# Cross-attention kernel on one core: column sums of probabilities folded on DVE and summed by one float32r matmul per tile in place of a float32 one

## The reference

```python
# emb (16, 100, 512), latent (16, 722, 256), weights 512x512 and 256x512
q = jnp.einsum('bte,ef->btf', emb, Wq) + bq
k = jnp.einsum('bml,le->bme', latent, Wk) + bk
v = jnp.einsum('bml,le->bme', latent, Wv) + bv
w = jnp.einsum('bte,bme->btm', q, k) * scale
w = jax.nn.softmax(w, axis=1)
pred = jnp.einsum('btm,bme->bte', w, v)
x = pred + emb
...
return (x - mu) * jax.lax.rsqrt(var + EPS) * gamma + beta
```

## Time and profile before

| | us |
|---|---|
| median of 3 runs | 142.18 (141.69 to 142.43) |
| the profiled execution | 141.24 |
| its span, first to last instruction | 139.4 |
| busy PE, DVE, ACT, POOL | 133.3, 103.0, 88.0, 78.6 |

### The profile page before, as it was taken

How to read it: one execution, slowest core, us unless ns; L and a number is a source line. 1 busy time by engine, 2 the same in 40 slices (tenths; PEclk the granted TensorE clock), 3 DMA queues, 4 the chain that set the end, 5 groups by cost and what they waited for, 6 DMA issues and landing times.

```text
span 139.4 us, 3004 instructions
## 1 busy us (share of the span) xinstructions
PE 133.3 (96%) x1042; PEld 128.8 (92%) x1042; DVE 103.0 (74%) x208; ACT 88.0 (63%) x299; POOL 78.6 (56%) x77
## 2 busy tenths in 40 slices
PE   7999999999999999999999999999999999999940
PEld 7899999999998999999999999999999999998930
DVE  0789995893545789579696955969596966797983
ACT  4366188989978753988292839565656637386320
POOL 0000005579984695646989272965476553639791
PEclk9999999999999999999999999999999999999997
DMA  4999999984287596978969899599787987535324
GB/s 146 336 397 419 416 260 398 345 302 177 51 292 269 174 360 186 397 258 307 273 266 339 265 333 377 187 356 334 270 252 240 325 277 236 224 111 212 115 75 150
DMA packets 10814, 37.33 MB, mean 268 GB/s; under 512 B 1200, under 2 KB 1456, under 8 KB 10800
## 3 DMA queue, kind: packets, MB, share of 16 engines
q1 hardware_dynamic: 9424, 34.79, 71.6%
q10 hardware_dynamic: 1376, 2.36, 4.6%
HBM read 33.87 MB, written 3.28 MB: 266 GB/s over the span
## 4 chain that ended last, share of the span: by engine, by line
PE 89%; POOL 5%; issue 2%; ACT 1%; POOLq 0%; DVE 0%; DVEq 0%
PE ps_S L427 29%; PE ps_U L441 27%; PE ps_Y L462 10%; PE ps_U L399 6%; PE ps_Y L399 6%; POOL xT_in L990 3%; PE ps_Y L342 2%; POOL xT_in L978 2%; PE ps_w L450 1%; PE ps_S L347 1%; PE ps_U L508 1%; PE ps_c L416 1%; PE ps_U L353 1%; ACT xT_in L626 1%; PE ps_U L358 1%
## 5 line engine op out<-in xcount | busy, mean ns | idle before, releaser
L608 ACT ACTIVATE expo<-scores,negmax 121x100 f32<-121x100 f32 x96 | 34.9, 365 | 22.0 <-DVE negmax L779 22.0
L427 PE MATMUL ps_S<-G,ctxT_in 128*121 128x100 f32 (+1 forms) x384 | 43.3, 269 | 0.0
L427 PEld LDWEIGHTS ps_S<-G,ctxT_in 128*121 128x121 f32 (+1 forms) x384 | 42.1, 185 | 0.0
L441 PEld LDWEIGHTS ps_U<-prob,ctx_in 121*128 121x128 f32 x336 | 39.4, 192 | 1.0
L441 PE MATMUL ps_U<-prob,ctx_in 121*128 121x100 f32 x336 | 39.6, 274 | 0.0
L789 DVE TENSOR_REDUCE probsum<-prob 121x100 f32<-121x600 f32 x16 | 19.8, 1239 | 6.0 <-POOL prob L967 5.7
L978 POOL TENSOR_TENSOR xT_in<-x_in,xT_in 128x512 f32<-128x512 f32 (+1 forms) x13 | 16.6, 1280 | 13.3 <-issue 9.8
L775 DVE TENSOR_TENSOR scores<-ps_S,c_rows 121x600 f32<-121x600 f32 x16 | 12.5, 781 | 15.6 <-issue 12.2
L967 POOL TENSOR_TENSOR prob<-expo,rinv 121x600 f32<-121x600 f32 x16 | 19.0, 1189 | 0.1
L608 ACT ACTIVATION_READ_ACCUMULATOR expo<-scores,negmax 121x1 f32 x96 | 18.0, 187 | 0.0
L990 POOL TENSOR_TENSOR xT_in<-wqk,beta_rows 128x512 f32<-128x512 f32 (+1 forms) x12 | 15.4, 1280 | 2.7 <-ACT wqk L634 2.7
(11 more groups left out here) (125 smaller groups left out, 202.4 us busy)
## 6 DMA issues: line engine op xcount, KB each, us to landing
ctx_in<-ctx SPq DMA_DIRECT2D x16, 768.0 KB, 5.2
ctxT_in<-ctxT SPq DMA_DIRECT2D x16, 722.0 KB, 5.0
xT_in<-xT SPq DMA_DIRECT2D x8, 400.0 KB, 8.7
x_in<-x SPq DMA_DIRECT2D x12, 256.0 KB, 4.5
out<-xT_in ACTq DMA_DIRECT2D x8, 256.0 KB, 3.7
wqk<-Wqk SPq DMA_DIRECT2D x4, 388.0 KB, 4.4
out<-xT_in SPq DMA_DIRECT2D x3, 256.0 KB, 2.0
wv_in<-Wv SPq DMA_DIRECT2D x1, 512.0 KB, 15.5
```

What stands on the lines that cost most here:

```text
L427: last = nc.tensor.matmul(ps_scores(c)[0:rows(c), :], ctxT_in[:, q, l * M + c * MP:l * M + c * MP + rows(c)], G[:, l, bass.ds(b * T, T)], ...
L441: last = nc.tensor.matmul(ps_U[:, q, l * T:(l + 1) * T], ctx_in[0:rows(c), q, c, l * P:(l + 1) * P], prob[0:rows(c), q, c * T:(c + 1) * T] ...
L608: last = nc.scalar.activation(expo[0:MP, q, c * T:(c + 1) * T], scores[0:MP, q, c * T:(c + 1) * T], ACT.Exp, bias=negmax[0:MP, q, c:c + 1] ...
```

## The change

weight_sum(j) now multiplies a new array sum_parts (128 partitions by 128 tokens, float32r, two buffers) by ones in one float32r matmul with two columns, in place of probsum by ones in float32 with one column. DVE makes sum_parts in three new instructions per tile: fold_sum(j) adds partitions 64 to 120 of probsum onto partitions 0 to 56 in place; upper_sum(j) copies the 64 folded rows, rounded to float32r, into partitions 0 to 63; lower_sum(j) subtracts that copy from the folded rows into partitions 64 to 127. The last tile's weight_sum stands on PE behind the values of the tile before it, not ahead of them.

```diff
+        sum_parts = sb("sum_parts", [P, 2, P], F32R)
...
             def weight_sum(j):
-                pe.wait_ge(probsum_set, last_batch(j) + 1)
+                pe.wait_ge(sum_parts_set, j + 1)
                 if j > 0:
                     pe.wait_ge(wsum_set, j)
-                nc.tensor.matmul(ps_w[0:tile_rows(j), 0:1], probsum[0:MP, tokens(j)], ones[0:MP, 0:1],
+                nc.tensor.matmul(ps_w[0:tile_rows(j), 0:2], sum_parts[:, j % 2, 0:tile_rows(j)], ones_r[:, 0:2],
                                  start=True, stop=True).then_inc(wsum_done, 1)
...
             late_U(1)
-            weight_sum(NT - 1)
...
             last.then_inc(Y_done, 1)
+            weight_sum(NT - 1)
             late_U(2)
...
+            def fold_sum(j):
+                dve.wait_ge(probsum_set, last_batch(j) + 1)
+                nc.vector.tensor_tensor(probsum[0:MP - P // 2, tokens(j)], probsum[0:MP - P // 2, tokens(j)],
+                                        probsum[P // 2:MP, tokens(j)], ALU.add).then_inc(sum_folded, 1)
+
+            def upper_sum(j):
+                dve.wait_ge(sum_folded, j + 1)
+                if j >= 2:
+                    dve.wait_ge(wsum_done, j - 1)
+                nc.vector.tensor_copy(sum_parts[0:P // 2, j % 2, 0:tile_rows(j)], probsum[0:P // 2, tokens(j)]).then_inc(sum_hi_set, 1)
+
+            def lower_sum(j):
+                dve.wait_ge(sum_hi_set, j + 1)
+                nc.vector.tensor_tensor(sum_parts[P // 2:P, j % 2, 0:tile_rows(j)], probsum[0:P // 2, tokens(j)],
+                                        sum_parts[0:P // 2, j % 2, 0:tile_rows(j)].bitcast(F32), ALU.subtract).then_inc(sum_parts_set, 1)
...
             def turn(b, q):
                 j = tile_of(b - 3)
+                i = tile_of(b - 2)
                 if exists(b - 3):
                     lower_U(b - 3, 1 - q)
+                if i is not None:
+                    fold_sum(i)
                 normaliser(b - 1, 1 - q)
+                if i is not None:
+                    upper_sum(i)
                 maxima(b, q)
+                if i is not None:
+                    lower_sum(i)
...
             normaliser(0, 0)
             maxima(1, 1)
             chunk_sum(0, 0)
+            fold_sum(0)
             normaliser(1, 1)
+            upper_sum(0)
+            lower_sum(0)
             maxima(2, 0)
```

More of the change, by code:

```diff
@@ L166, in xattn @@
         probsum_set = sem("probsum_set")
+        sum_folded = sem("sum_folded")
+        sum_hi_set = sem("sum_hi_set")
+        sum_parts_set = sem("sum_parts_set")
         U_done = sem("U_done")
@@ L870, in _ @@
             chunk_sum(1, 1)
+            fold_sum(1)
             maxima(3, 1)
+            upper_sum(1)
             normaliser(2, 0)
+            lower_sum(1)
             dve.wait_ge(rows_in, 48)
@@ L883, in _ @@
             chunk_sum(3, 1)
+            fold_sum(2)
             centre(1)
+            upper_sum(2)
             lower_U(2, 0)
+            lower_sum(2)
             normaliser(4, 0)
@@ L895, in _ @@
             lower_U(B - 4, 0)
+            fold_sum(NT - 3)
             normaliser(B - 2, 0)
+            upper_sum(NT - 3)
             maxima(B - 1, 1)
+            lower_sum(NT - 3)
             add_residual(NT - 4)
@@ L900, in _ @@
             chunk_sum(B - 2, 0)
+            fold_sum(NT - 2)
             aggregate(NT - 4)
+            upper_sum(NT - 2)
             lower_U(B - 3, 1)
+            lower_sum(NT - 2)
             normaliser(B - 1, 1)
@@ L924, in _ @@
             chunk_sum(B - 1, 1)
+            fold_sum(LAST)
             add_residual(NT - 3)
+            upper_sum(LAST)
             late_lower(1)
+            lower_sum(LAST)
             row_stats(NT - 3)
```

## The result

The changed kernel takes 148.57 us (median; 147.92 to 148.98) against 141.95 (141.68 to 142.43) measured beside it: ratio 1.0476, 95% interval 1.0447 to 1.0506. The forecast was 150.4 us, in a range of 144.5 to 153.5, and a difference of +8.3 us; the difference is +6.6. Of every kernel, executions over 1.5% above its fastest are left out of medians and ratios.

The account below looks back on a forecast made before the run. PE's gapless matmuls bound the kernel; 4.5 + 0.5 (busy turns) + 1.3 (early) + 3.1 (tail) - 1.1 (PE's gain) = +8.3 us, so 150.4 us for the median, range 144.5 to 153.5.

Parts of the forecast that it names:

- What bounds, and the sign: PE's matmuls, busy 96% of the span, bound the kernel; the change makes it slower, chance 0.84.
- The fold and the lower part wait for the end of a POOL instruction: DVE's new two-SBUF-input instructions, coming second, wait for POOL's whole instruction; fold 1.3 to 1.6 us instead of 0.30.
- The cast waits as a whole: DVE's upper part also waits for POOL's instruction, 1 us instead of 0.22; case of both kinds waiting: chance 0.50.
- The rival in which it doesn't: Only the two-input DVE instructions wait, the cast doesn't: +0.85 us a turn, +5.0 in all, 147.2 us; chance 0.25.
- Turns 7, 11 and 12 at 1.5 us each, plus 0.5: Busy turns behind another busy turn: PE loses 1.5 us each, 4.5 together, and 0.5 more in turn 7.
- The 0.5 for L1006 and L1009: Turn 7: two POOL additions of 1.0 us each behind the probabilities catch the lower part, +0.5 us.
- Turns 8 and 13 ... turns 9 and 14: Turns without a tile of b - 2, or without values: DVE catches up there, PE's earlier loss stays.
- Early, 1.3 us: fold(0) waits behind POOL's Wv_lo, delaying DVE by up to 2 us; 1.3 us (0 to 3) reaches PE in turns 4 to 6.
- Tail, 3.1 us: From turn 15 on, waits of fold, cast and lower part delay DVE's L816 from 129.75 to 132.9: +3.1 us.
- PE's gain, 1.1 us: One float32r pass saves 0.11 us per weight sum, ten of 13 sums before the last scores end: -1.1 us.
- The last weight sum ... hidden: Moved behind values(11) on PE, it is ready at about 132.2, its residual wanted at 133.7: no cost.
- PE: gaps ... ahead of values: Expected sign in the profile: PE gaps of 1 to 2 us ahead of values in turns 8, 12 and 13.

Follow-up runs that it names:

- e4: Kernel before, with one float32r two-column matmul per weight sum on a constant array of ones, no new DVE work: 139.90 us, ratio 0.9894.
- e10: Kernel before, with the chunk sum itself writing float32r and one float32r matmul per weight sum, lower parts left out: 140.37 us, ratio 0.9907.
- e1: Changed kernel with fold, cast and lower part each turned into a one-input tensor_reduce over an axis of length one: 142.48 us, ratio 1.0070.
- e2: Changed kernel with only the cast turned into a tensor_reduce over an axis of length one: 146.98 us, ratio 1.0364.
- e7: Changed kernel with tile 0 summed the old way (float32, no new DVE instructions): 149.31 us, ratio 1.0557.
- e11: Changed kernel measured once more without any edit, in another set of runs: 148.73 us, ratio 1.0524.
- e6: Changed kernel with the last two tiles, 11 and 12, summed the old way (float32, no new DVE instructions): 145.96 us, ratio 1.0314.
- e3: Changed kernel with fold and lower part turned into tensor_reduces over an axis of length one, the cast kept: 142.63 us, ratio 1.0077.
- e8: Changed kernel with the three DVE instructions of tiles 1 to 10 moved behind the completing chunk sum, tiles 0, 11, 12 the old way: 144.02 us, ratio 1.0174.
- e9: As e8, but with the instructions of tiles 3, 6 and 10 moved behind the next turn's lower_U: 146.88 us, ratio 1.0384.

## Why the prediction was right, and where it was off

- **What bounds, and the sign: right.** PE was the bound, its gain is about 1% (e4, e10), and DVE's new work made it wait.
- **The fold and the lower part wait for the end of a POOL instruction: right**, and shown by the rows and by e1. "The fold in busy turns: 1.3 to 1.6 us long" was too long: it took 1.07 to 1.12.
- **The cast waits as a whole: right** (1.17 us). The rival in which it doesn't falls. e2's 146.98 is close to the 147.2 of that rival, which was its time for exactly that kernel.
- **Turns 7, 11 and 12 at 1.5 us each, plus 0.5: oversized.** Net of the 0.11 for PE the forecast is 1.9, 1.4 and 1.4, together 4.7; measured, as what values of turns 8, 12 and 13 lose, are 1.5, 0.8 and 1.2, together 3.5. DVE's turn came out at 8.0 us, not 8.3, mostly because the residual began 0.15 us earlier beside lower_U than on before's clock and the fold took 1.12 instead of 1.33 us. Turn 13 shows the price without margin, 1.2 + 0.1 = 1.3 = 8.0 - 6.7. Turn 12 lost 0.4 less: I read that as margin which turns 6 and 10 had not eaten, the lower part of turn 10 having taken 0.67 us where I had it wait for the whole of the probabilities; no run tests that. The 0.5 for L1006 and L1009 was about right: the lower part of turn 7 took 0.67 us, 0.4 over its own time.
- **"Turns 8 and 13 ... turns 9 and 14": one term is missing.** I had PE lose nothing there. The weight sum of turn 9 waits for a lower part which the probabilities hold, and 0.3 us are lost, 0.4 to 0.5 before PE's gain.
- **Early, 1.3 us: the size about right, the reason wrong, so luck.** The sum went by fold(0) behind Wv_lo, and e7 shows that this costs nothing. Behind the start, values of turn 7 are 0.5 us late, and those of e4 0.6 us early: 1.1 us are lost (1.6 in e11's trace). About 0.9 of them is there in e1 too, by turn 6: it is DVE's work without any wait, which the prediction let fit into idle time everywhere but in the tail.
- **Tail, 3.1 us: right** (3.0, and e6). Its last steps, in the form of the earlier trace rows:
```profile
132.44 1.24 DVE L793 TENSOR_REDUCE probsum<-prob 121x100 f32<-121x600 f32 x1 [0.48 <-POOL prob L1012]
133.71 1.31 DVE L798 TENSOR_TENSOR probsum<-probsum 57x128 f32<-57x128 f32 x1
134.95 0.68 DVE L822 TENSOR_TENSOR ps_Y<-ps_Y,xT_in 128x512 f32<-128x512 f32 x1
...
135.55 0.68 DVE L805 CAST sum_parts<-probsum 64x128 fp32r<-64x128 f32 x1
...
137.70 0.15 DVE L836 TENSOR_SCALAR vareps<-meanvar 128x1 f32<-128x1 f32 x1
```
```profile
132.36 2.51 POOL L1023 TENSOR_TENSOR xT_in<-x_in,xT_in 128x512 f32<-128x512 f32 x2
134.84 1.32 POOL L1035 TENSOR_TENSOR xT_in<-wqk,beta_rows 128x512 f32<-128x512 f32 x1
```
  The fold is held by the second residual and the cast by the finish; from the chunk sum to L836 it is 5.26 us, where it was 3.65. About half of the tail's price is no wait: the tail of e1 is 1.4 us longer than that of the kernel before.
- **PE's gain, 1.1 us: right or somewhat small.** 1.5 and 1.3 us in e4 and e10, whose intervals overlap. The 0.11 us a sum was the middle of two bounds with little to support it, and it came out exactly (6.83 to 6.72). By the values of turn 15 e4 is 1.3 us ahead; 0.3 more come in the tail, which the forecast left out.
- **"The last weight sum ... hidden": right, by little.** The bias made from it is ready at 138.01 and POOL takes it up at 138.45, behind rstd: 0.4 us, where I had 1.5. The chain of waits passes through it there.
- **"PE: gaps ... ahead of values": right in the main.** The three named gaps are there; 1.3 us stand ahead of weight sums, as the view above says.

The terms as measured, net of PE's gain and behind the start, are 0.5 early, 1.5, 0.8 and 1.2 in the three turns, 0.3 around turn 9 and 3.0 in the tail, less 0.2 in the other turns: +7.1 us. The forecast +8.3 came near it through errors of both signs.

What stays open: how far a late start of the projections lasts, and so a few tenths of every term before turn 7; and what DVE's idle time is worth in the turns before turn 6, where no run moves one tile's instructions alone.

## What to carry to other kernels

An engine's idle time is no room for an instruction that shares a path with a neighbour: look up who is running at the moment at which it will ask, and price it at the rest of that instruction. A wait of 1 us on an engine with 1.3 us of slack costs nothing by itself (e3), and once two or three of them meet in a turn what goes beyond the slack is paid in full; moving the work to where the neighbour is idle helps only if the same place also has slack behind it (e8), and the move shifts the neighbour as well (e9). Where a result may be rounded, let the instruction that makes it write the type that the matmul wants.

## What the runs showed of the hardware

- Short instructions wait as long as long ones. 57 partitions by 128 columns of two SBUF inputs take 0.29 us free and 1.12 under a POOL instruction of 1.27 us; 57 by 64 took 2.31 us under one of 2.37. In nearly all of these waits the blocked instruction ends 0.12 to 0.17 us sooner after the release than its own time would say.
- A float32 to float32r cast waits too: 0.21 us free and 1.17 blocked for 64x128, 1.90 for 64x64 in e3. The Trainium skill (SBUF — State Buffer, "Who interferes with whom") says so of copies in a two-port mode; here the trace now agrees, with these numbers.
- A tensor_reduce over an axis of length one, 57x128, took 281 ns, and never over 282 in all 13 places, also in the middle of a POOL instruction (68.24 in e1): a copy that doesn't wait. In place of the cast of 64x128 it takes 0.26 us against 0.21. The Trainium skill (the same section) says that tensor_reduce never contends on trn2; the trace agrees.
- One float32r weight sum in place of a float32 one gave back 0.11 us a turn (6.83 to 6.72), and a tensor_reduce that writes float32r costs what one that writes float32 does.
